# Shorter runs in the key and value loads, and the row of maxima sent by four DMAs from SBUF to SBUF

## What is computed

```
q, k, v = split(layernorm(x) @ wqkv + bqkv)            # 49 windows (7 x 7) of 64 tokens
idx = top_k(mean(q) @ mean(k).T, 4)                    # each window chooses 4 windows
kg, vg = k[idx], v[idx]                                # 256 keys and values for each window
scores = einsum('brqhd,brkhd->brhqk', qh, kh) * scale  # 8 heads of 8
attn = softmax(scores)
x = x + (einsum('brhqk,brkhd->brqhd', attn, vh) @ wo + bo)
x = x + gelu(layernorm(x) @ w1 + bm1) @ w2 + bm2
```

## Time and profile before

| | us |
|---|---|
| median of 3 runs | 5539.94 |
| the runs | 5518.09 to 5563.86 |
| span of the profiled execution (first to last instruction) | 5568.0 |
| TensorE busy | 4677.0 |
| VectorE busy | 3447.6 |
| ScalarE busy | 3285.4 |
| GpSimd busy | 2747.0 |

### The profile page before, as it was taken

One profiled execution on the slowest core, in us unless ns is written; L12 is line 12 of the kernel. 1 busy time (PEld: TensorE's weight loads), 2 busy tenths in 40 slices (PEclk: granted clock), 3 DMA queues, 4 the chain that ended last, 5 costly groups with the idle time before them and its releaser, 6 DMA issues.

```text
span 5568.0 us, 230234 instructions
## 1 busy us (share of the span) xinstructions
PE 4677.0 (84%) x68754; PEld 3217.0 (58%) x68754; DVE 3447.6 (62%) x7969; ACT 3285.4 (59%) x6282; POOL 2747.0 (49%) x9656
## 2 busy tenths in 40 slices
PE   2388888888889888888888888888888888888888
PEld 1265565656556565565656656565565656556564
DVE  2266666666666666666666666666566666667665
ACT  1156556565665656556565665656556565665656
POOL 1245455454544545445454554545455454554553
PEclk8589999998998999889989999989899999989999
DMA  1333343333333333333333423333343333323311
GB/s 53 102 98 92 83 109 76 100 77 96 102 77 98 84 95 91 82 103 80 94 83 91 111 72 103 81 96 92 79 109 79 96 81 102 100 75 102 84 40 33
DMA packets 627124, 487.33 MB, mean 88 GB/s; under 512 B 483792, under 2 KB 613968, under 8 KB 615536
## 3 DMA queue, kind: packets, MB, share of 16 engines
q10 hardware_dynamic: 335360, 205.62, 16.4%
q1 hardware_dynamic: 290416, 265.73, 16.2%
HBM read 262.38 MB, written 208.73 MB: 85 GB/s over the span
## 4 chain that ended last, share of the span: by engine, by line
PE 45%; DMA 18%; issue 10%; SPq 7%; ACT 7%; DVE 5%; DVEq 3%; POOL 2%; ACTq 2%; POOLq 1%
DMA max_d<-tr 11%; PE ps L988 9%; PE ps L1002 7%; PE ps L1019 7%; PE ps L881 4%; DMA qm<-qk_d 3%; PE ps L938 3%; DMA xin<-in_x 3%; DVEq L223 2%; DVE mx L724 2%; SPq L327 2%; PE ps L949 2%; PE ps L901 2%; ACT hid L813 2%; PE ps L974 2%
## 5 line engine op out<-in xcount | busy, mean ns | idle before, releaser
L724 DVE TENSOR_REDUCE mx<-ps 128x4 f32<-128x1024 f32 x1568 | 1921.7, 1226 | 1702.3 <-PE ps L988 1354.0
L832 ACT ACTIVATE pt<-ps 128x512 f32<-128x512 f32 x3136 | 1694.3, 592 | 869.2 <-PE ps L1002 814.4
L506 POOL COPY vg<-vs 64x64 f32 x6272 | 1526.5, 243 | 782.0 <-POOL kg L490 576.7
L988 PE MATMUL ps<-kg,qm 96*128 96x256 f32 x6272 | 1336.2, 338 | 386.6 <-DVE mx L724 127.3
L490 POOL CAST kg<-ks 96x128 fp32r x3136 | 851.0, 297 | 1511.6 <-PE ps L1002 1156.6
L988 PEld LDWEIGHTS ps<-kg,qm 96*128 96x128 f32 x6272 | 946.8, 202 | 1053.6 <-issue 889.5
L1002 PE MATMUL ps<-qm,kg 97*128 97x256 f32 x6272 | 1119.8, 301 | 178.8 <-ACT pt L832 102.3
L1019 PE MATMUL ps<-pt,vg 128*32 128x64 f32 x50176 | 1091.4, 231 | 0.0
L1002 PEld LDWEIGHTS ps<-qm,kg 97*128 97x128 f32 x6272 | 926.2, 203 | 252.2 <-ACT pt L832 164.8
L1019 PEld LDWEIGHTS ps<-pt,vg 128*32 128x32 f32 x50176 | 826.1, 115 | 224.2 <-issue 34.8
L643 DVE CAST kg<-ks 96x128 fp32r x3136 | 625.6, 241 | 126.2 <-issue 123.5
(11 more groups left out here) (109 smaller groups left out, 3866.7 us busy)
## 6 DMA issues: line engine op xcount, KB each, us to landing
qk_d<-stg SPq DMA_DIRECT2D x224, 448.0 KB
qm<-qk_d ACTq DMA_DIRECT2D x1792, 42.0 KB
ks<-qk_d ACTq DMA_DIRECT2D x96, 784.0 KB, 6.2
vs<-v_d ACTq DMA_DIRECT2D x64, 784.0 KB, 6.7
xin<-in_x SPq DMA_DIRECT2D x119, 224.0 KB
xi_d<-xi SPq DMA_DIRECT2D x112, 224.0 KB
qk_d<-stg SPq DMA_DIRECT2D x112, 224.0 KB
max_d<-tr SPq DMA_DIRECT2D x1568, 2.0 KB
```

The source lines that it names most:

```text
L506: j = pool.tensor_copy(dst.rearrange("p j (e x) -> p j e x", e=2)[:, :, :, 0:HD], vs[place(m)[0]][rows, bass.ds(region, 1), :].rearrange(" ...
L724: v.tensor_reduce(mx[h % 2][:].rearrange("p (g j e) -> p g j e", g=2, j=2)[:, :, :, 0], ps[:, 0:2, :].rearrange("p g (j k) -> p g j k", j= ...
L832: act.activation(pt[m % 2][:, c], ps[:, 2 + c, :], ACT.Exp, scale=float(HD) ** -0.5).then_inc(S["pt_ready"], 1)
L988: i = pe.matmul(ps[:, g, 256 * j:256 * j + 256], qm[c % 2][0:NP3, t, g, 2 * j:2 * j + 2, :].rearrange("p h t -> p (h t)"), kg[slot][0:NP3, ...
```

## The change

- The key and value loads are issued with a largest run of 1792 bytes (`PIECE`), so each row of 12544 bytes goes in seven pieces. The keys of an image come in six DMAs in place of three (each half of the channels by itself), the values in two as before: eight (`KV_DMAS`) in place of five. The second image's loads go out one each step from step 6 on, the first image's every second step from step 70 on, as before.
- `max_d`, the hop, the row DMA and the semaphores `hopped` are gone. In the step of the transpose, after its wait for `tr_ready`, SyncE issues four DMAs, one for each `j`, from four partitions of `tr` (32 apart, 128 bytes each) straight to 512 bytes of the row in `qm`. Each adds 16 to `row_ready`, so TensorE waits for 64 a step.
- `tr` has seven buffers in place of two. VectorE's wait for the hop before the reduction is gone; before the transpose it waits for the row of seven steps ago.

```diff
-KV_DMAS = 5
+KV_DMAS = 8
+PIECE = 4 * ST
...
-        max_d = dram("max_d", (RING, HEADS // 2, 128))
...
-        tr = [sb(f"tr{i}", [128, 32]) for i in range(2)]
+        tr = [sb(f"tr{i}", [128, 32]) for i in range(RING)]
...
         def keys_values(eng, q, i, n):
 
-            if n < 3:
-                src = qk_d[bass.ds(q, 1), i, C:2 * C, n // 2, :].rearrange("o (g c) n -> (o c) g n", g=NG)
-                dst = ks[i][n:NP3:3].rearrange("p g r t -> p g (r t)").bitcast(F32)
+            if n < 6:
+                slot, g = n // 2, n % 2
+                src = qk_d[bass.ds(q, 1), i, C + 32 * g:C + 32 * g + 32, slot // 2, :].rearrange("o c n -> (o c) n")
+                dst = ks[i][slot:NP3:3, g].rearrange("p r t -> p (r t)").bitcast(F32)
             else:
                 src = v_d[bass.ds(q, 1), i].rearrange("o t r n -> (o t) (r n)")
-                dst = vs[i][64 * (n - 3):64 * (n - 3) + 64].rearrange("p r n -> p (r n)")
-            eng.dma_start(dst, src).then_inc(kv_loaded[i], 16)
+                dst = vs[i][64 * (n - 6):64 * (n - 6) + 64].rearrange("p r n -> p (r n)")
+            eng.dma_start(dst, src, max_dma_last_dim=PIECE).then_inc(kv_loaded[i], 16)
...
-                if 0 <= local - B_LOAD < 2 * KV_DMAS and (local - B_LOAD) % 2 == 0:
-                    keys_values(eng, p if kind == "lead" else p + 1, 1, (local - B_LOAD) // 2)
+                if 0 <= local - B_LOAD < KV_DMAS:
+                    keys_values(eng, p if kind == "lead" else p + 1, 1, local - B_LOAD)
...
-                m = h - 1
-                if live(m, kind):
-
-                    sp.wait_ge(hopped[m % 2], (p * R + m // 2 + 1) * 16)
-                    settled(sp)
-                    sp.dma_start(qm[m // NW % 2][NP3:NP3 + 1, m % NW].rearrange("o g h t -> o (g h t)").bitcast(F32),
-                                 max_d[m % RING].rearrange("j p -> (j p)").unsqueeze(0)).then_inc(row_ready[m % RING], 16)
                 if live(h, kind):
 
                     sp.wait_ge(S["tr_ready"], T + 1)
                     settled(sp)
-                    sp.dma_start(max_d[h % RING].rearrange("j (b n) -> b j n", n=32), tr[h % 2][0:128:8, :]).then_inc(hopped[h % 2], 16)
+                    for j in range(HEADS // 2):
+                        row = qm[c % 2][NP3:NP3 + 1, t, j // 2, 2 * (j % 2):2 * (j % 2) + 2].rearrange("o h t -> o (h t)")
+                        sp.dma_start(row.bitcast(F32), tr[h % RING][8 * j:128:32, :]).then_inc(row_ready[h % RING], 16)
...
                     v.wait_ge(S["sm_full"], T + 1)
-                    if live(h - 2, kind):
-                        v.wait_ge(hopped[h % 2], (p * R + (h - 2) // 2 + 1) * 16)
...
                     v.wait_ge(S["mx_ready"], T + 1)
                     settled(v)
-                    v.transpose(tr[h % 2][:], mx[h % 2][:]).then_inc(S["tr_ready"], 1)
+                    if live(h - RING, kind):
+                        v.wait_ge(row_ready[h % RING], (p * 14 + h // NW) * 64)
+                    v.transpose(tr[h % RING][:], mx[h % 2][:]).then_inc(S["tr_ready"], 1)
...
-                pe.wait_ge(row_ready[slot], (p * 14 + c + 1) * 16)
+                pe.wait_ge(row_ready[slot], (p * 14 + c + 1) * 64)
```

## The result

The change makes the kernel slower: 5943.86 us (median of 4 runs, 5932.76 to 5956.09) against 5540.12, a ratio of 1.0734 (95% interval 1.0698 to 1.077). The forecast was 5410, faster by 2.3%; the range ended at 5700.

What follows compares the result with a forecast made beforehand. SyncE's round, waiting for its own DMAs, was taken as close to the bound. Per pair -7.5, -6.5 and +5.1 made -8.9 us; 15 pairs' worth, -134 from 5568, gave 5434, as a median 5410; range 5240 to 5700.

Steps and rivals of the forecast that it cites:

- What bounds the kernel: Opening part: PE is busy 84% of the span; SyncE's round, waiting for its own previous DMA, is close to the bound.
- SyncE's issue time: Deciding term, steps 18 to 63: 3.23 us a step with four DMAs; steps 42 to 59 +5.1 us a pair.
- the line through two rows by number of partitions: Price of a new DMA's issue: line through hop (541 ns) and routing indices (812 ns), 440 ns at four partitions.
- formula 1.47 + 4x: SyncE's time in us for a step in steps 18 to 63, x being the issue time of one new DMA.
- What is late next: Part on what delays the kernel after the change: SyncE's issue time, in steps 18 to 63 with the strip's stores.
- the others have a step time above 3.23 or few stores: Reason in the issue-time term for adding no cost in steps outside 28 to 59.
- The gain beside the loads: Steps 7 to 17 fall to 39.4 us (-7.5), steps 70 to 76 to 23.2 (-6.5), a pair.
- Loads in pieces: Part on key and value loads: shorter pieces and half-size key DMAs reduce the 3.9 us delay of the maxima.
- half or less, since a key load has half the bytes: Assumed remaining share of the 3.9 us delay behind a load; no row shows how far it falls.
- SyncE as the bound: Rival, steps 28 to 59: at 541 ns an issue, +18 us a pair; x from 0.48 to 0.6 had chance 0.25.
- point of decision, 0.51 us: Issue time x at which the SyncE-bound rival's loss in steps 28 to 59 equals the 14 us a pair gained.
- rule on small transfers: Rival from the Trainium skill: coalesce small transfers; four in a row estimated at 8 us a step; no separate chance given.

Runs made afterwards that it cites:

- e6: The kernel before, loads whole, with SyncE issuing this step's hop first, then the last step's row, and seven transposed tiles: 5634.62 us, ratio 1.0153.

## Why the prediction was wrong

- **What bounds the kernel** was read rightly in part. With one DMA in place of the hop, the row and the wait, steps 42 to 59 fall from 53.0 to 50.0 us. That it is SyncE's round, the wait for its own DMA, isn't shown: `e6` takes that wait away and only moves it.
- **The term SyncE's issue time** was mis-sized. The step that failed is the line through two rows by number of partitions, 440 ns; the issues cost 500, and 16 partitions cost no more than four. The nearest row itself, the hop's 541, was the better price. The formula 1.47 + 4x holds: with 0.50 it gives 3.47 us a step, 48.6 us for steps 28 to 41 and 62.5 for 42 to 59, measured 49.3 and 64.1. This is 9 us a pair of the miss (14.4 by the formula against the forecast's 5.1): 7.7 from the price, the rest because steps 28 to 41 were taken at 45.1 us from one pair, where the mean is 43.7.
- **What is late next** was looked for in steps 28 to 59 alone. The step that failed stands in the sum, "the others have a step time above 3.23 or few stores". Steps 60 to 69 and 84 to 97 take 16.1 us a pair more (3.1 + 6.3 + 6.7), the largest part of the miss and in no rival. In steps 63 to 69 SyncE is full as well (0.04 us of wait in 4.07). In steps 84 to 97 it has time to spare, but an engine that isn't full can still deliver late: the load of x stands behind four issues, 2.1 us in place of the hop's 0.5, and ScalarE waits for it in order. Of the 16.1 us the load of x issued first gives back 9.5 (3.2 + 6.3) and two value tiles 4.1, in steps 60 to 62; the pieces have a part in the 6.7, since alone they cost those steps 3.8. The shares beyond these were not taken apart.
- **The gain beside the loads** was twice too large: -7.1 us a pair against -14. The step that failed took the step time of stretch 84 to 97, 3.31 us, for steps 7 to 17. Even with one DMA a step and no full SyncE they take 42.5 us, 3.9 a step, so there is more in that stretch than the hop: the last strips of a pair and the loop's turn stand there, but what it is was not taken apart. Steps 70 to 76 stop at 25.8 us, and at 24.7 with one DMA, against the forecast's 23.2.
- **Loads in pieces**: the forecast's "half or less, since a key load has half the bytes" was the right rule for key loads, 5.5 to 3.2 us, but the value loads keep their bytes and their delay, and the spreading alone only moved the cost (-4.0 us in steps 70 to 76, +3.8 in steps 84 to 97). The rule of the Trainium skill that stood beside it ("DMA: Bandwidth & Descriptors", "Queues, rings and completion order": an engine leaves a queue only at the end of a packet of several descriptors) agrees with the 3.0 and 3.2 us for whole and cut rows; how many descriptors a packet held no run shows.
- **The rivals.** SyncE as the bound was the right one; its point of decision, 0.51 us, lay above the 0.50 that came, because it counted the strip's steps 28 to 59 and nothing behind them; even its time at 541 ns, some 5600, lies 340 us below the 5943.86 that came at 500. The Trainium skill's rule on small transfers ("DMA: Bandwidth & Descriptors", "Rules for kernel authors": coalesce) spoke on the right side: four issues of 500 ns against one of 493. The 8 us a step estimated from that page did not come; a step of steps 42 to 59 took 3.56.
- VectorE's wait for the hop is gone and the new one before the transpose costs nothing, as forecast: neither is in the list of waits.

The sum, a pair: -8.9 forecast, +9.3 (issues), +16.1 (steps 60 to 69 and 84 to 97), +6.9 (less gain beside the loads) make +23.4; measured +24.9.

What part of the strip's loss is the granted clock, 0.909 before and 0.891 now as a mean, was not taken apart.

## What to carry to other kernels

Count a DMA by its issue, not by its bytes: on SyncE one small DMA cost half a microsecond whether it took four partitions or sixteen, so four in place of two are 1.2 us a step. When a queue gets more to issue in a step, list what stands behind it in that step and who waits for that, also where the queue isn't full. To let small transfers past a large load, cut the load into DMAs with fewer bytes and space them; cutting its rows did not help here. Spacing moves the last parts later: look at what they meet there.

## What the runs showed that was not expected

- The cost of an issue did not grow with the partitions: 500, 576 and 493 ns for 4, 8 and 16 source partitions into one, while a run already contiguous in DRAM cost 228.
- A load of 784 KB in runs of 1792 bytes delayed a small DMA on another queue as long as one in runs of 12544: 6.8 and 6.7 us after value loads, 5.6 and 5.3 where no other load was near.
- Taking 1461 us of waits for the hop from SyncE (1621.4 to 159.9) made the kernel 1.5% slower: 1435 us came back as its wait for the transposed tile.
- The place of the load of x in SyncE's step was worth 146 us, two thirds of it in steps in which SyncE waits 30% of the time (1.14 of 3.80 us).
